# Image 0's first attention in two halves of its queries, the half scores and exponentials among the row maxima

## The reference

```python
q, k, v = wq @ xf, wk @ xf, wv @ xf          # 32 x 1024 per image
att = softmax(einsum('bmi,bmj->bij', k, q), axis=2)
x = x + wo @ einsum('bij,bmj->bmi', att, v)  # attention 1
t = tokens(x)
t = t + softmax(n(t) @ n(t).T) @ n(t)        # attention 2, n: layer norm
t = t + moe(n(t))                            # router softmax, top 2 of 8 experts
```

## Time and profile before

| | us |
|---|---|
| median of 3 runs (226.16 to 229.27) | 226.32 |
| the profiled execution | 226.99 |
| its span, first to last instruction | 225.3 |
| TensorE busy | 206.7 |
| VectorE busy | 143.6 |
| ScalarE busy | 107.4 |
| GpSimd busy | 62.5 |

### The profile page before, as it was taken

One profiled execution on the slowest core, in us unless ns is written; L12 is line 12 of the kernel. 1 busy time (PEld: TensorE's weight loads), 2 busy tenths in 40 slices (PEclk: granted clock), 3 DMA queues, 4 the chain that ended last, 5 costly groups with the idle time before them and its releaser, 6 DMA issues.

```text
span 225.3 us, 2932 instructions
## 1 busy us (share of the span) xinstructions
PE 206.7 (92%) x1075; PEld 105.0 (47%) x1075; DVE 143.6 (64%) x358; ACT 107.4 (48%) x166; POOL 62.5 (28%) x75
## 2 busy tenths in 40 slices
PE   7899899998999887989997999899999999898993
PEld 2554443653643333544443534434445433376873
DVE  2589864587509854472589468936784272698970
ACT  2631664397684473176543623685645566301110
POOL 8140000053211200003002445830177751017260
PEclk9999999999999999699999999999999999999999
DMA  4752000000000000000000000010000002000021
GB/s 104 143 144 44 3 0 0 0 1 3 1 0 0 0 3 0 0 0 0 3 0 1 0 3 0 1 47 0 3 0 0 0 3 48 0 0 3 0 47 47
DMA packets 3341, 3.67 MB, mean 16 GB/s; under 512 B 2176, under 2 KB 2432, under 8 KB 3328
## 3 DMA queue, kind: packets, MB, share of 16 engines
q1 hardware_dynamic: 3328, 3.50, 7.0%
HBM read 2.45 MB, written 1.05 MB: 16 GB/s over the span
## 4 chain that ended last, share of the span: by engine, by line
PE 69%; DVE 18%; ACT 7%; issue 2%; DMA 2%; POOL 1%; SPq 0%; DVEq 0%; POOLq 0%
PE acc L490 25%; DVE rowmax L1070 7%; PE ring L596 7%; PE ring L551 6%; PE ring L483 6%; PE ring L552 5%; PE ring L465 4%; PE acc L626 3%; DMA xin<-in_x 2%; PE ring L454 2%; PE ring L455 2%; ACT prob L880 2%; DVE qst L1062 2%; DVE stats L1103 1%; ACT prob L877 1%
## 5 line engine op out<-in xcount | busy, mean ns | idle before, releaser
L880 ACT ACTIVATE prob<-ring,shift 128x1024 f32<-128x1024 f32 x32 | 35.6, 1112 | 35.0 <-PE ring L552 34.9
L1070 DVE TENSOR_REDUCE rowmax<-ring 128x1 f32<-128x1024 f32 x32 | 37.6, 1218 | 11.6 <-PE ring L465 11.6
L877 ACT ACTIVATE prob<-ring 128x1024 f32<-128x1024 f32 x32 | 32.0, 1025 | 16.3 <-PE ring L483 16.3
L368 POOL TENSOR_TENSOR sm<-sm,minus_half 128x8 f32<-128x8 f32 x8 | 15.8, 1974 | 84.5 <-DVE sm L1113 84.5
L490 PE MATMUL acc<-prob,u 128*64 128x512 f32 x128 | 32.5, 627 | 1.0 <-ACT prob L880 1.0
L490 PE MATMUL acc<-prob,val 128*64 128x512 f32 x128 | 31.1, 605 | 1.0 <-ACT prob L877 1.0
L551 PE MATMUL ring<-zst 128*128 128x512 f16 x64 | 24.6, 384 | 3.8 <-DVE rowmax L1070 2.7
L465 PE MATMUL ring<-qst,kst 96*128 96x512 f32 x64 | 22.4, 439 | 2.0 <-DVE kst L1067 1.0
L552 PE MATMUL ring<-zsw,zst 128*128 128x512 f16 x64 | 24.3, 379 | 0.0
L1209 DVE TENSOR_TENSOR prod<-ring,gate 128x1024 f32<-128x1024 f32 x16 | 19.4, 1220 | 7.3 <-PE ring L596 6.8
L483 PE MATMUL ring<-kst,qst 98*128 98x512 f32 x64 | 20.8, 423 | 3.0 <-DVE kst L1083 1.2
(11 more groups left out here) (155 smaller groups left out, 311.3 us busy)
## 6 DMA issues: line engine op xcount, KB each, us to landing
xin<-in_x SPq DMA_DIRECT2D x8, 256.0 KB, 4.0
out<-ob SPq DMA_DIRECT2D x6, 128.0 KB, 2.3
e_in<-in_L_ffn_expert_w SPq DMA_DIRECT2D x2, 128.0 KB
out<-ob SPq DMA_DIRECT2D x4, 64.0 KB, 2.0
eb_in<-in_L_ffn_expert_b SPq DMA_DIRECT2D x8, 2.0 KB
wo<-in_L_conv_wo SPq DMA_DIRECT2D x2, 8.0 KB, 2.4
r_in<-in_L_ffn_router_w SPq DMA_DIRECT2D x2, 2.0 KB
w<-in_L_conv_wq SPq DMA_DIRECT2D x1, 16.0 KB, 3.5
```

Source lines behind the costliest of these rows:

```text
L368: pool.tensor_tensor(sm[:, 3, :], sm[:, 2, :], minus_half[:, :], ALU.pow).then_inc(s_rs, 1)
L877: act.activation(prob1[:, j % DEEP, :], flat(filled(act, f"st{j}", b)), ACT.Exp).then_inc(s_p1, 1)
L880: act.activation(prob2[:, j % DEEP, :], flat(filled(act, f"s{j}", b)), ACT.Exp, bias=shift[:, :], accum_out=rsum2[b % 2][:, j:j + 1]).then ...
L1070: dve.tensor_reduce(rowmax[:, tile:tile + 1], flat(filled(dve, f"mx{tile}", b)), AX.X, ALU.max).then_inc(s_mx, 1)
```

## The change

Image 0's first attention is split by queries. The even tiles (first 512 columns of `kst`) are half 0, the odd ones half 1. The maxima are taken in the order 0, 2, 4, 6, 1, 3, 5, 7 (`BY_HALF`). After four of them `negate_half(0)` negates those, `max_row_half(0)` turns them by four matmuls, and ScalarE copies the row. Then `scores1_half(0, g)`, for g from 0 to 3, makes the scores of the tiles 2g and 2g + 1 against the 512 queries of half 0 (two matmuls, one ring place, `ha0` to `ha3`), and one exponential of 2 x 512 columns writes them into `prob1`, which now has 8 slots. They stand among the scores for the maxima of tiles 3, 5 and 7. Half 1 follows behind the second row (`hb0` to `hb3`), and only then is a pair weighed. The projection of k of image 1 moves from the head to behind `hb0`, the values of image 1 move ahead of `mx7` of image 1, and the fillers are placed anew. All other images keep their code, with two more on the counts of `s_nm`.

```diff
-DEEP = 4
+DEEP1 = 8
+DEEP2 = 4
+BY_HALF = [0, 2, 4, 6, 1, 3, 5, 7]
...
-HEAD = [("w3", 0), ("q", 0), ("k", 0), ("vx", 0)] + per_tile("mx", 0) + [("q", 1), ("k", 1), ("mr", 0)]
-FIRST = [("st0", 0), ("st1", 0), ("mx0", 1), ("st2", 0), ("mx1", 1), ("st3", 0), ("mx2", 1), ("mx3", 1), ("st4", 0),
-         ("mx4", 1), ("st5", 0), ("mx5", 1), ("st6", 0), ("mx6", 1), ("st7", 0), ("mx7", 1), ("vx", 1), ("mr", 1),
-         ("po", 0)]
+HEAD = [("w3", 0), ("q", 0), ("k", 0), ("vx", 0), ("mx0", 0), ("mx2", 0), ("mx4", 0), ("mx6", 0), ("mx1", 0), ("mr0", 0),
+        ("ha0", 0), ("mx3", 0), ("ha1", 0), ("mx5", 0), ("ha2", 0), ("mx7", 0), ("ha3", 0), ("q", 1), ("mr1", 0)]
+FIRST = [("hb0", 0), ("k", 1), ("hb1", 0), ("hb2", 0), ("mx0", 1), ("mx1", 1), ("hb3", 0), ("mx2", 1), ("mx3", 1),
+         ("mx4", 1), ("mx5", 1), ("mx6", 1), ("vx", 1), ("mx7", 1), ("mr", 1), ("po", 0)]
...
+            def max_row_half(half):
+                buf = take(f"mr{half}", 0)
+                pe.wait_ge(s_nm, 2 * (half + 1))
+                for tile in range(half, T, 2):
+                    c = col(tile)
+                    mm = pe.matmul(flat(buf)[0:ROW + 2, c:c + P], nmax[:, tile, :], ident_r[:, :], start=True, stop=True)
+                mm.then_inc(s_fill, 1)
+            def scores1_half(half, g):
+                buf = take(("ha", "hb")[half] + str(g), 0)
+                if g == 0:
+                    pe.wait_ge(s_mrow, half + 1)
+                for n in range(2):
+                    j = 2 * g + n
+                    mm = pe.matmul(buf[:, n, :], qst[0][0:ROW + 2, col(j):col(j) + P],
+                                   kst[0][0:ROW + 2, chunk(half)], start=True, stop=True)
...
+            max_scores(0, 1)
             pe.wait_ge(s_wol, 2 * 16)
             pe.transpose(acc2[:, 0:C], wo4[:, :, :].rearrange("p a m -> p (a m)"), ident[0:C, 0:C]).then_inc(s_woT, 1)
+            keep_clock(2)
+            max_row_half(0)
+            scores1_half(0, 0)
+            for g in range(1, 4):
+                max_scores(0, 2 * g + 1)
+                scores1_half(0, g)
+                keep_clock(2)
             project_qk("q", 1)
+            max_row_half(1)
+            keep_clock(2)
+            scores1_half(1, 0)
             project_qk("k", 1)
-            keep_clock(3)
-            max_row(0)
-            keep_clock(3)
+            scores1_half(1, 1)
+            weigh_pair1(0, 0)
+            scores1_half(1, 2)
             max_scores(1, 0)
...
@@ ScalarE @@
             round_x(1)
+            buf = filled(act, "mr0", 0)
+            act.activation(kst[0][ROW:ROW + 2, 0:CHUNK], buf[ROW:ROW + 2, 0, :], ACT.Copy).then_inc(s_mrow, 1)
...
+            for g in range(4):
+                exp1_half(0, g)
             round_q(1)
+            exp1_half(1, 0)
             round_k(1)
...
@@ VectorE @@
-            for tile in range(T):
-                row_max(0, tile)
             dve.wait_ge(s_const, 4)
-            negate_max(0)
+            for half in range(2):
+                for tile in BY_HALF[4 * half:4 * half + 4]:
+                    row_max(0, tile)
+                negate_half(half)
+            buf = filled(dve, "mr1", 0)
+            dve.tensor_copy(kst[0][ROW:ROW + 2, CHUNK:N], buf[ROW:ROW + 2, 1, :]).then_inc(s_mrow, 1)
             split_q(1)
-            max_row(0)
             split_k(1)
```

More of the change, by code:

```diff
@@ L267, in release @@
                 return table[name]
+            if name in ("mr0", "mr1"):
+                return s_mrow, int(name[-1]) + 1
+            if name[:2] == "ha":
+                return s_ha, int(name[-1]) + 1
+            if name[:2] == "hb":
+                return s_p1, 2 * int(name[-1]) + 2
+            if name[:2] == "mx" and b == 0:
+                return s_mx, BY_HALF.index(int(name[-1])) + 1
             family, at = {"mx": s_mx, "st": s_p1, "s": s_p2, "e": s_prod}[name[:-1]], int(name[-1])
@@ L485, in scores1, with weigh @@
                 mm.then_inc(s_fill, 1)
-            def weigh(acc, stationary, prob, j, s_p, s_sum, b):
+            def weigh(acc, stationary, prob, deep, j, s_p, s_sum, b):
                 pe.wait_ge(s_p, T * b + j + 1)
                 for h in range(2):
-                    mm = pe.matmul(acc[h * C:(h + 1) * C, :], stationary[:, j, :], prob[:, j % DEEP, h * CHUNK:(h + 1) * CHUNK],
+                    mm = pe.matmul(acc[h * C:(h + 1) * C, :], stationary[:, j, :], prob[:, j % deep, h * CHUNK:(h + 1) * CHUNK],
                                    start=(j == 0), stop=(j == T - 1))
@@ L876, in exp1 @@
             def exp1(b, j):
-                act.activation(prob1[:, j % DEEP, :], flat(filled(act, f"st{j}", b)), ACT.Exp).then_inc(s_p1, 1)
+                act.activation(prob1[:, j % DEEP1, :], flat(filled(act, f"st{j}", b)), ACT.Exp).then_inc(s_p1, 1)
             def exp2(b, j):
-                act.activation(prob2[:, j % DEEP, :], flat(filled(act, f"s{j}", b)), ACT.Exp, bias=shift[:, :],
+                act.activation(prob2[:, j % DEEP2, :], flat(filled(act, f"s{j}", b)), ACT.Exp, bias=shift[:, :],
                                accum_out=rsum2[b % 2][:, j:j + 1]).then_inc(s_p2, 1)
@@ L941, in _, with exp1_half @@
             round_x(1)
+            buf = filled(act, "mr0", 0)
+            act.activation(kst[0][ROW:ROW + 2, 0:CHUNK], buf[ROW:ROW + 2, 0, :], ACT.Copy).then_inc(s_mrow, 1)
+            def exp1_half(half, g):
+                buf = filled(act, ("ha", "hb")[half] + str(g), 0)
+                probs = act.activation(prob1[:, 2 * g:2 * g + 2, chunk(half)], buf[:, :, :], ACT.Exp)
+                if half:
+                    probs.then_inc(s_p1, 2)
+                else:
+                    probs.then_inc(s_ha, 1)
+            for g in range(4):
+                exp1_half(0, g)
             round_q(1)
+            exp1_half(1, 0)
             round_k(1)
-            max_row(0)
-            for j in range(4):
-                exp1(0, j)
+            exp1_half(1, 1)
+            exp1_half(1, 2)
+            exp1_half(1, 3)
             act.wait_ge(s_ew, (5 + T) * 16)
             act.activation(e1[:, :], e_in[:, :, :].rearrange("p e c -> p (e c)"), ACT.Copy).then_inc(s_er, 1)
-            act.wait_ge(s_const, 4)
+            act.wait_ge(s_const, 5)
             for h in range(2):
@@ L1076, in negate_max, with negate_half @@
                 dve.tensor_scalar(hi, rm, -1.0, None, ALU.mult).then_inc(s_nm, 1)
-                dve.wait_ge(s_nm, 2 * b + 1)
+                dve.wait_ge(s_nm, 2 * b + 3)
                 dve.scalar_tensor_tensor(out=nmax[:, :, ROW + 1:ROW + 2], in0=rm, scalar=-1.0, in1=hi.bitcast(F32),
+                                         op0=ALU.mult, op1=ALU.subtract).then_inc(s_nm, 1)
+            def negate_half(half):
+                dve.wait_ge(s_mx, 4 * (half + 1))
+                hi = nmax[:, half:T:2, ROW:ROW + 1]
+                rm = rowmax[:, half:T:2].unsqueeze(2)
+                dve.tensor_scalar(hi, rm, -1.0, None, ALU.mult).then_inc(s_nm, 1)
+                dve.wait_ge(s_nm, 2 * half + 1)
+                dve.scalar_tensor_tensor(out=nmax[:, half:T:2, ROW + 1:ROW + 2], in0=rm, scalar=-1.0, in1=hi.bitcast(F32),
                                          op0=ALU.mult, op1=ALU.subtract).then_inc(s_nm, 1)
```

35 lines of the change are left out of this document (13 added, 22 removed).

## The result

The changed kernel took 231.55 us (median of 4, 230.29 to 231.88) beside 226.33 us for the kernel before: ratio 1.022, 95% interval [1.0188, 1.0253]. That is 5.2 us slower, outside the range on record.

A forecast was written before the change was run, and what follows sets the result against it. TensorE (92% busy) was taken to bound the span on average, with VectorE's row maxima setting the pace in image 0's head. Waits of +0.2 us and a clock fall of +1.5 us on 226.3 gave 228.0 us, range 225.6 to 229.9.

The forecast's parts named there:

- The head, step by step: Image 0's maxima and handovers: VectorE idle 1.5 us before tile 3, half scores at 19.88 and 27.15 without a clock fall.
- The half rate in the head: At the moved handover, from about 20.1 us: thin TensorE use likely halves the clock for 3.4 us, +1.5 us, bounds 0 and 1.7.
- no fall in the head: Rival: fillers and dense issue keep the clock up at the moved handover, only waits count, 226.5 us; chance 0.25.
- The waits behind the head: From the second half's scores to image 1's first weighing: new waits against work done early, +0.2 us in all without the clock.
- half of the delay: At image 1's first scores, 0.5 us late: half is hidden, so the first weighing starts at 48.83 for 48.62.
- The late fall: Half rate from about 91.7 to 95.1 us in the kernel before: 3.4 us long, 1.7 us lost, inside the measured span.
- the case of 228.0: Main case: one clock fall in the head, 226.3 + 1.7 = 228.0 us, with 227.2 to 228.8; chance 0.42.
- two more falls: Rival: another fall at the second half's handover, seen in 28 to 34 us, +1.7 us, 229.7 us; chance 0.20.
- third fall: A further clock fall at another thin place (71 to 74 us), reaching 231.4 us; a quarter of 0.20 lay above 230.9.
- a fall later disappears: Rival: the fall at 91.7 us may not come once work shifts, giving 1.7 us back, 226.3 or 224.8 us; chance 0.13.

The follow-up runs named there:

- late fillers alone: Changed kernel with 5 fillers behind image 0's attention-2 scores of tile 7 and 2 behind the next scores for image 2's maxima: 228.38 us, ratio 1.0089.
- the kernel before without its fillers: Kernel before without the 12 fillers among image 0's maxima, nothing else changed: 229.29 us, ratio 1.0136.
- the changed kernel with both fillers: Changed kernel with 6 more fillers ahead of the first half row, 4 behind it, and 5 and 2 in the late idle places: 226.79 us, ratio 1.0018.
- the one before with late fillers: Kernel before with 5 fillers behind image 0's attention-2 scores of tile 7 and 2 behind the next scores for image 2's maxima: 225.66 us, ratio 0.996.
- the second set: Changed kernel run again unaltered, 8 executions: 227.71 us (227.25 to 231.46), ratio to the kernel before 1.0076.
- all 18: All executions of the unaltered changed kernel, from its three sets of 4, 8 and 6: median 229.3 us.
- the first set: First four executions of the unaltered changed kernel, the value on record: 231.55 us (230.29 to 231.88), ratio to the kernel before 1.022.
- head fillers: Changed kernel with 6 more fillers ahead of the first half row and 4 between it and the first half scores: 229.09 us, ratio 1.0112.
- the shifted one: Kernel before with 13 more fillers between image 0's row of maxima and the first transposed scores: 229.80 us, ratio 1.0185.
- the third set: Changed kernel run a third time unaltered, 6 executions: 229.32 us (227.19 to 231.56), ratio to the kernel before 1.0119.

## Why the prediction was wrong

- **The head, step by step: right.** VectorE's idle ahead of tile 3 (1.5 forecast, 1.52), the first half scores (19.88 forecast, 20.27 less the 0.42 of the start), the second half's (28.6 with a fall forecast, 29.04 less 0.42), all within 0.1 us.
- **The half rate in the head: right in place and size.** 1.5 us forecast, 1.4 measured; the four traces of kernels with the gap uncovered (the changed kernel three times, and with late fillers alone) have it, and so has the kernel before without its fillers; none of the other nine has. The longest idle ahead of it in the changed kernel was 1.29 us. The Trainium skill ("TensorE: Matmul & The Clock Gate", "A second HAM failure mode: psum-queue depth-cycling") says that frequent short idles between groups of matmuls are enough to make the clock fall and rise, and the trace agrees. The rival *no fall in the head* falls with it.
- **The waits behind the head: mis-sized.** +0.2 us forecast, 0.8 measured. Two terms. Image 1's first scores were to be 0.5 us late and were 1.0 late (47.70 in the changed kernel with both fillers, 46.69 in the one before with late fillers), since its last maximum was 0.7 behind the forecast. A part of that is pairs of scores behind a weighing, which I priced at 0.47 and which take 0.58 (33.61 to 34.19 and 37.08 to 37.66 in the changed kernel; the trace of before has it too, 34.78 to 35.36); the rest was not traced step by step. And half of the delay was called hidden, where 0.8 of the 1.0 us passes on.
- **A term that the sum had at nothing: an addition on VectorE, 0.3 us.** The output projection comes later against GpSimd's subtraction for image 2, and VectorE's addition behind it now starts second of the two and takes 2.53 us instead of 0.69. VectorE is then busy when ScalarE has rounded the next q (54.36 + 1.02 = 55.38), and splits it 0.4 us later, where before it stood waiting for it; TensorE's next scores (57.05, 54.03 before) wait for that split. The split is 4.49 us behind the first weighing, before 4.14. That is the 0.3 us that all kernels with the halves have from the first weighing to the end (175.4 for 175.1). First the changed kernel, then the kernel before:

```profile
50.23 2.35 POOL L386 TENSOR_TENSOR xst<-xin,xst 64x1024 fp32r<-64x1024 f32 x1 [32.65 <-ACT xst L889]
...
54.36 1.02 ACT L892 ACTIVATE qst<-ring 96x1024 fp32r<-96x1024 f32 x1 [1.39 <-PE ring L456]
...
55.78 1.22 DVE L1108 TENSOR_TENSOR qst<-ring,qst 32x1024 fp32r<-32x1024 f32 x1
```

```profile
47.47 0.69 DVE L1096 TENSOR_TENSOR tok<-tdiv,xt 128x512 f32<-128x512 f32 x1
47.57 2.82 POOL L374 TENSOR_TENSOR xst<-xin,xst 64x1024 fp32r<-64x1024 f32 x1 [30.61 <-ACT xst L854]
...
52.76 1.22 DVE L1062 TENSOR_TENSOR qst<-ring,qst 32x1024 fp32r<-32x1024 f32 x1 [1.09 <-ACT qst L857]
```

- **The late fall, taken to stay as it is in the case of 228.0: the step that failed.** I treated the late half rate as one of 3.4 us that either stays or goes. It can also double, with the work merely shifted: 6.8 us of half rate from 93.4 to 100.2 in place of 3.4, which was 1.6 us here, in a place that no case of mine named. My *two more falls* put the extra one at 28 to 34 us, where the clock stayed at 1.00; that its third fall reached 231.4, beside 231.55 measured, is chance. The rival *a fall later disappears* did come about in the second set's trace (none late, 227.29 us), so the fault is to have left out the doubling, not to have thought the late stretch movable.
- **The start.** 0.4 us of the difference between the two profiles, and 1.1 between two executions of the changed kernel (12.68 and 13.79), come from half rate ahead of the first maximum. It is not of the change, and was not in the sum.
- **The level.** What the change did in each of its three traces is 0.8 + 1.4 + 0.3 = 2.5 us (2.25 and 0.3 in the first), for 1.7 forecast. The rest of the recorded 5.2 depends on where half rate falls in an execution; the first of the first four had it doubled, and the mean clock of the others (0.970 to 0.977) says the same or nearly. The middle of all 18, 229.3 us, is 3 us over the kernel before, inside the range; the value on record is not, and I had no case of 4 in 10 executions above 230. Two sums of mine were rounded loosely (18.7 for 18.6 us of work, 2.1 for 2.0 of idle); that is 0.1 us.

What stays open: why the first set met the upper group four times, and what in the filling of a half-rate stretch decides whether it doubles.

## What to carry to other kernels

Splitting a stage to start its successor early pays only if no engine's list puts the successor's handover ahead of work that the bottleneck of the moment still needs: here one pair of matmuls one place too late left VectorE idle for 1.5 us, and moving it gave 0.7 back. Where a handover leaves TensorE thinly used, price the clock with the waits, and cover the idle with fillers if they are free; they were worth 1.4 us in the head and up to 3.2 late, the order some 1.2. A shift can also let two engines meet that had missed each other, as the slow addition shows. And if a profile shows a half-rate stretch anywhere, a shift of the work ahead of it is not neutral: take several sets of executions, group them by granted clock, and compare stretches between fixed marks of the traces rather than medians.

## What the runs showed of the hardware

- Every stretch in which the granted clock was 0.50 and that ended inside the span lasted 3.4 or 6.8 us. Late, it lasted 6.8 us where 11 or more of the 16 short value matmuls came behind the fall (the changed kernel, with and without head fillers, the kernel before without fillers, and the shifted one), and 3.4 us where 3 or none did and weighing matmuls filled it (the kernel before, the third set). That the filling is the reason is read from where the matmuls lie; it was not varied by itself, and one double stretch in a head had no short matmuls in it.
- An addition on VectorE of two operands in SBUF took 2.53 us (50.61, L1152, above) instead of 0.69 us while GpSimd ran its own subtraction from 50.23 to 52.58. In the kernel before it had started first and took 0.69, and GpSimd's took 2.82 us for 2.35. So it was in all 14 traces: 2.53 to 2.73 us where GpSimd had started first, 0.69 where VectorE had.
- At the start of a program the granted clock of the trace can read 1.00 while matmuls go at half pace: 0.43 us apart from 8.33 to 9.6 us in the kernel before, 0.23 after.
